# Score and maxima products of an attention in four column groups of TensorE

## The reference

```
x   = x + conv_attention(x)             # full softmax over 1024 x 1024, keys of 16 channels
a   = layer_norm(tokens(x))
g   = global attention(a)               # 8 heads of 16, 1024 x 1024 scores per head
l   = local attention(a)                # 4 heads of 32, window of 5
a   = layer_norm(a + fuse2(silu(fuse1([g, l]))))
a   = layer_norm(a + ffn2(silu(ffn1(a))))
t   = tokens(x) + a
out = t + mixture of 8 experts(layer_norm(t))    # top 1, capacity 1280
```

## Time and profile before

| | before |
|---|---|
| median of three runs | 1690.2 us |
| profiled execution, its own time | 1695.85 us |
| its span, first to last instruction | 1694.1 us |
| granted clock of TensorE, mean | 0.952 |
| busy: PE, PEld, DVE, ACT, POOL | 1547.7, 785.7, 1310.9, 1005.3, 723.0 us |
| maxima products L1604 | 1024, 395 ns each |
| score products L1623 | 1024, 389 ns each |
| value matmuls L1635 | 2048, 616 ns each |
| the chain that ended last: PE, DVE, ACT, DMA | 63%, 17%, 7%, 5% |

### The profile page before, as it was taken

How to read it: one execution, slowest core, us unless ns; L and a number is a source line. 1 busy time by engine, 2 the same in 40 slices (tenths; PEclk the granted TensorE clock), 3 DMA queues, 4 the chain that set the end, 5 groups by cost and what they waited for, 6 DMA issues and landing times.

```text
span 1694.1 us, 24958 instructions
## 1 busy us (share of the span) xinstructions
PE 1547.7 (91%) x8475; PEld 785.7 (46%) x8475; DVE 1310.9 (77%) x2791; ACT 1005.3 (59%) x1907; POOL 723.0 (43%) x1126
## 2 busy tenths in 40 slices
PE   7778999999999999999999999999989988879993
PEld 4524334544454344434543454435533432449992
DVE  5487898789788988897877878897868762638984
ACT  2302756667766776677656667676666576315543
POOL 4203311126542564346433544644565356224562
PEclk8867999999999999999999999999999998979996
DMA  2355640152225222422144212421163111033335
GB/s 74 111 135 172 231 130 10 36 178 72 79 83 150 64 82 82 136 77 82 48 130 117 82 58 99 118 94 54 60 166 100 67 38 47 7 89 110 106 119 215
DMA packets 122899, 165.38 MB, mean 98 GB/s; under 512 B 14134, under 2 KB 86891, under 8 KB 122772
## 3 DMA queue, kind: packets, MB, share of 16 engines
q1 hardware_dynamic: 115284, 153.60, 29.9%
q0 software_dynamic: 4608, 7.30, 1.3%
q10 hardware_dynamic: 2880, 2.88, 0.5%
HBM read 104.41 MB, written 61.15 MB: 98 GB/s over the span
## 4 chain that ended last, share of the span: by engine, by line
PE 63%; DVE 17%; ACT 7%; DMA 5%; issue 3%; POOL 3%; SPq 1%; POOLq 0%; ACTq 0%; DVEq 0%
PE bank L1635 11%; PE bank L1604 9%; PE bank L1623 9%; PE bank L1557 7%; DVE gmax L2274 6%; PE bank L1869 4%; PE bank L1474 4%; DVE cmax L2207 3%; PE bank L1549 2%; PE bank L1672 2%; ACT prob L1997 2%; PE bank L1662 2%; DMA kv_d<-lqkv 2%; PE bank L1578 1%; DMA gparts_d<-parts 1%
## 5 line engine op out<-in xcount | busy, mean ns | idle before, releaser
L1997 ACT ACTIVATE prob<-bank 128x512 f32<-128x512 f32 x1024 | 572.3, 596 | 283.0 <-PE bank L1623 281.0
L2274 DVE TENSOR_REDUCE gmax<-bank 128x1 f32<-128x512 f32 x1024 | 656.3, 681 | 61.5 <-PE bank L1604 59.0
L1604 PE MATMUL bank<-k_stack,q_stack 96*128 96x512 bf16 x1024 | 398.1, 395 | 32.8 <-DVE gmax L2274 15.7
L1623 PE MATMUL bank<-q_stack,k_stack 99*128 99x512 bf16 x1024 | 391.7, 389 | 24.9 <-ACT prob L1997 18.0
L1635 PE MATMUL bank<-prob,v_tok 128*32 128x512 f32 x2048 | 277.8, 616 | 0.0
L1604 PEld LDWEIGHTS bank<-k_stack,q_stack 96*128 96x128 bf16 x1024 | 100.7, 99 | 258.6 <-DVE gmax L2274 142.2
L1381 POOL TENSOR_TENSOR lprod<-ls,kv_win 128x640 f32<-128x640 f32 x64 | 81.0, 1287 | 270.2 <-DVE ls L2333 270.2
L1623 PEld LDWEIGHTS bank<-q_stack,k_stack 99*128 99x128 bf16 x1024 | 99.8, 99 | 190.7 <-ACT prob L1997 121.1
L1374 POOL TENSOR_TENSOR lprod<-ql_tok,kv_win 128x640 f32<-128x640 f32 x64 | 99.6, 1577 | 136.7 <-DMA ql_tok<-ql_d 135.9
L1557 PEld LDWEIGHTS bank<-cv_tok,cprob 128*128 128x128 f32 x960 | 114.4, 192 | 21.9 <-DVE t_tok L2241 11.3
L1557 PE MATMUL bank<-cv_tok,cprob 128*128 128x129 f32 x960 | 121.1, 279 | 1.3 <-DVE t_tok L2241 0.4
(11 more groups left out here) (294 smaller groups left out, 2558.2 us busy)
## 6 DMA issues: line engine op xcount, KB each, us to landing
kv_win<-kv_d SPq DMA_DIRECT2D x32, 1280.0 KB, 5.7
kv_d<-lqkv SPq DMA_DIRECT2D x64, 128.0 KB, 3.0
gparts_d<-cprob SPq DMA_DIRECT2D x24, 256.0 KB
gparts_d<-parts SPq DMA_DIRECT2D x24, 256.0 KB
q_stack<-gparts_d SPq DMA_DIRECT2D x32, 192.0 KB, 3.2
k_stack<-gparts_d SPq DMA_DIRECT2D x16, 384.0 KB, 5.5
rows_d<-rows SPq DMA_DIRECT2D x10, 528.0 KB, 5.8
cprob<-rows_d SPq DMA_DIRECT2D x8, 660.0 KB, 5.5
```

The source lines that it names most:

```text
L1604: mm(max_ps[max_bank(n)][:, :], q_stack[quad][0:KROWS, h, i * P:(i + 1) * P], key_slot(b, quad)[0:KROWS, h, j * HN:(j + 1) * HN], start=Tr ...
L1623: mm(score_ps[n % 2][:, :], key_slot(b, quad)[0:KM, h, j * P:(j + 1) * P], q_stack[quad][0:KM, h, half * HN:(half + 1) * HN], start=True, ...
L1997: nc.scalar.activation(prob[:, g % 2, h, :], score_ps[n % 2][:, :], ACT.Exp).then_inc(exp_made, 1)
L2274: v.tensor_reduce(gmax[:, h, i, j:j + 1], max_ps[max_bank(n)][:, :], AX.X, ALU.max)\
```

## The change

The four heads' value products already go to four column groups. The change issues each maxima and score product in the same way: a new function, `by_columns`, cuts the 128 weight columns into four of 32 (`CG`) and issues four matmuls with the same moving operand, each writing 32 partitions of the same bank. The semaphore's increment sits on the last of the four; the waits ahead of the first stay. The result in the bank, its readers and all other engines' instructions are the same. PE instructions of these products go from 2048 loads and 2048 matmuls to 8192 of each.

```diff
--- before.py
+++ after.py
@@ -1601,14 +1601,20 @@
                 if n % (TILES // 2) == 0:
                     after(pe, queries_in[quad][n // (TILES // 2)], (b + 1) * 3 * 16)
                 h, i, j = max_at(n)
-                mm(max_ps[max_bank(n)][:, :], q_stack[quad][0:KROWS, h, i * P:(i + 1) * P],
-                   key_slot(b, quad)[0:KROWS, h, j * HN:(j + 1) * HN], start=True, stop=True).then_inc(max_full, 1)
+                by_columns(max_ps[max_bank(n)], q_stack[quad][0:KROWS, h, i * P:(i + 1) * P],
+                           key_slot(b, quad)[0:KROWS, h, j * HN:(j + 1) * HN]).then_inc(max_full, 1)
 
             def guard(b, quad):
                 max_fill(b, quad, TILES)
                 after(pe, guard_step, (b * 2 + quad + 1) * NEG_STEPS)
                 turn(max_ps[max_bank(TILES)][:, :].bitcast(BF16)[0:3 * QH * NT, 0:P],
                      gneg_parts[:, :, :].rearrange("p s t -> p (s t)"), identity=identb[:, :]).then_inc(max_full, 1)
+
+            def by_columns(ps, weights, moving):
+
+                for c in range(0, P, CG):
+                    last = mm(ps[c:c + CG, :], weights[:, c:c + CG], moving, start=True, stop=True)
+                return last
 
             def score_tile(b, quad, n):
                 u = b * 2 * TILES + quad * TILES + n
@@ -1620,8 +1626,8 @@
                     after(pe, guard_in[quad], (b + 1) * 48)
                 g, h = n // QH, n % QH
                 half, j = g // NT, g % NT
-                mm(score_ps[n % 2][:, :], key_slot(b, quad)[0:KM, h, j * P:(j + 1) * P],
-                   q_stack[quad][0:KM, h, half * HN:(half + 1) * HN], start=True, stop=True).then_inc(score_full, 1)
+                by_columns(score_ps[n % 2], key_slot(b, quad)[0:KM, h, j * P:(j + 1) * P],
+                           q_stack[quad][0:KM, h, half * HN:(half + 1) * HN]).then_inc(score_full, 1)
 
             def pv_group(b, quad, g):
```

## The result

| | before | after |
|---|---|---|
| median | 1691.6 us (4 runs) | 1753.4 us (4 runs, 1751.1 to 1759.0) |
| ratio, 95% interval | | 1.0356 (1.0324 to 1.0388) |
| span of the profiled execution | 1694.1 us | 1757.3 us |
| granted clock, mean | 0.952 | 0.949 |

The change makes the kernel 3.6% slower: +62 us, where +75 was forecast (1765, range 1715 to 1830).

A forecast was written before the change was run, and what follows sets the result against it. TensorE's own stream was taken to bound the kernel. Borders (+78) and first loads (+42) add 120 us, pauses absorb 45: 1695.85 + 120 - 45 = 1771, less 5.7 to the runs' median, 1765 us; range 1715 to 1830.

The forecast's parts named there:

- A product in four: Maxima or score product as four matmuls side by side: 0.22 us as before; bounds 0.215 and 0.43.
- the prediction's first rival: TensorE's product in four is dear: about 62 ns per matmul or a 25 ns floor; chance 0.15 for over 0.24 us.
- its 164 us: Weight loads of products in four, 107 ns per product instead of 27 if unhidden; left out of the sum.
- Borders: TensorE's changes between full width and column groups: 591 stays instead of 253 at 0.23 us each, +78 us.
- stay: Run of matmuls in column groups between wide ones on TensorE; priced 0.09 + 0.14 = 0.23 us.
- First loads: First weight load behind a stay, not drawn ahead over the border: 0.06 or 0.10 us each, +42 us.
- Pauses: TensorE's 95 us of standing still, mostly waits for a bank, absorb 45 us of new work; bounds 10 and 95.
- A dear product: Rival: eight instructions in 0.22 us overload TensorE's queue, or loads aren't hidden; 1826 to 2195 us, chance 0.15.
- Full absorption: Rival: TensorE's pauses take nearly everything, 95 us absorbed, ending at 1715 us; chance 0.10.
- A border dear only on the f32 side: Rival: a border costs only where its column side is f32, so the kernel gets faster, 1632 us; chance 0.04.
- Matmuls one behind the other: Rival: a product's four matmuls don't run side by side on TensorE, 1310 us more; chance 0.01.
- The signs: Expected in the trace: products 0.22 apart, value groups 0.86 between products, conv products 0.33 with two borders, shorter ScalarE and VectorE pauses.

The follow-up runs named there:

- experiment 3: The change with each product in eight matmuls (512 moving columns cut in halves) or 16 (quarters), instead of four: 1756.4 us and 1855.1 us.
- experiment 1: Against the kernel before, only the score products or only the maxima products in four column groups, the others at full width: 1833.6 us and 1794.5 us.
- experiment 4: The change with maxima and score products in two groups of 64 weight columns instead of four of 32; value products keep 32: 1794.2 us, ratio 1.056.
- experiment 5: Kernel before, with each step that may take either form given full width or four column groups by a dynamic programme over TensorE's order: 1679.4 us, ratio 0.9912.
- maxima alone: Against the kernel before, only the 1024 maxima products in four column groups, scores at full width: 1794.5 us, ratio 1.059.
- scores alone: Against the kernel before, only the 1024 score products in four column groups, maxima at full width: 1833.6 us, ratio 1.080.

## Why the prediction was right

- **A product in four costs 0.22.** Right: 0.22 in the trace, and experiment 3 shows room to at least twice the instructions. The upper bound of 0.43 was never near. 4, 8 and 16 matmuls all take 0.22 to 0.23 per product, down to 14 ns each, so neither price per matmul that the prediction's first rival weighed binds a product here. The loads stay hidden as it assumed; its 27 ns for the load of a full-width product, and so its 164 us, stand on no row.
- **Borders.** The mechanism was right (experiments 1, 4 and 5), the count of 591 stays as well. The price of a stay, 0.23 us, was taken from a value group and is too high for a product: 0.091 in and 0.100 out. The value group's 1.00 holds another 0.02 between its two passes (0.453 instead of 0.430 from start to start), which a group with products in four ahead of it doesn't pay. +64.6 us, not +78. This is the term that was mis-sized.
- **First loads.** Estimated at +42, measured at +39.7 by the ledger.
- **Clock.** A change of it isn't in the sum; the ledger has +5 us, within what executions differ by.
- **Pauses.** 45 us booked, 45.6 found. The amount was a choice between 10 and 95, so that it fits is luck in good part. Where the pauses went shows at the islands. From a product over one conv product to the next product it is 0.45 at the shortest before and 0.74 after, but in the median 0.62 and 0.75 (98 and 90 such places at the full clock): over half of these places had a pause, and the borders and loads take its place. Experiment 1 shows what a share can't: the pauses gave up to about 60 us there and no more.
- Together 64.6 + 39.7 + 5.1 - 45.6 = 64 against 120 - 45 = 75. The 11 us too many are 13 of borders (the price of the stay) and 2 of first loads, less the 5 of the clock.
- **The rivals.** A dear product: out by the trace and by experiments 1 and 3. Full absorption: out, 131 us of pauses remain. A border dear only on the f32 side: out by experiment 1. Matmuls one behind the other: out, a product would take 0.86.
- **The signs.** Most came as written: 0.22 within a stay, 0.86 for a value group with products on both sides, a border on each side of a conv product. "Shorter pauses for ScalarE and VectorE" did not, if it means their own: both idle longer (318 and 87 us, from 283 and 62), since they have the same work in a longer span.
- **A slip in the range.** 45 us absorbed, give or take 40, gives 1725 to 1805, not 1728; nothing else hangs on it.

Not settled is what TensorE does in the 0.09 to 0.10 us of a border. That it empties before the form changes would fit all runs, and none shows it. That the first load behind a border isn't drawn ahead is read from distances alone; no kernel took that cost away by itself.

## What to carry to other kernels

Count the places in TensorE's order where the form of the weights changes between full width and column groups, or between groups of different width; here each costs 0.09 to 0.10 us, and up to 0.10 more for the f32 load behind it. Splitting a full-width product of 512 moving columns into column groups is free in itself here, so use it to join neighbouring stretches of narrow products, not to make an island between wide ones. Where kinds alternate, as scores and maxima do here, converting one of them is worse than both or none, and the choice can be computed from the order.

## What the runs showed that I had not expected

- 16 loads and 16 matmuls in 0.23 us run at 7 ns per instruction from start to start, but not for long: with 39195 matmuls in the program, TensorE stopped 42 times ahead of products, for up to 3.6 us, without a wait that the profile names. With 22811 it stopped 3 times (3.6 us in all).
- TensorE's pauses, by the ledger, are a cushion with a floor in these runs: 176 us before, 131, 114, 117 and 112 us with 109, 159, 207 and 163 us of new work (the change, maxima alone, scores alone, two groups).
- The form of the f32 matmuls of conv and the tail is as free as that of the bf16 products: 0.11 a pass with 129 moving columns, 0.43 with 512.
